# One shared stationary tile for the last 48 columns of gate and up, and a full 128-row last step of down

## The chip, the cores and the metric

The kernel runs on one core of one Trainium2 chip. The metric is the device time of one execution in microseconds (us). Shorter is better. TensorE appears in the profile as PE (matrix products) and PEld (loads of the stationary operand), VectorE as DVE, ScalarE as ACT, GpSimd as POOL, and the queue that issues DMAs as SP.

## What is computed

The kernel holds one layer: a gated delta-rule attention, then a feed-forward part. Input x has 4 sequences of 1024 tokens with 256 values, so 4096 tokens. Cut to the ends and the feed-forward part, the reference is

```python
x = x + _layernorm(attention(_layernorm(x), ...))
x = x + _layernorm(_L0_ffn_ref(_layernorm(x), lut, gate_idx, up_idx, down_idx))

def _L0_ffn_ref(x, lut, gate_idx, up_idx, down_idx):
    gate = x @ lut[gate_idx].T      # 256 -> 688
    up = x @ lut[up_idx].T          # 256 -> 688
    h = silu(gate) * up
    return h @ lut[down_idx].T      # 688 -> 256
```

The layer norm subtracts the mean and divides by the root of the variance plus 1e-5, with no weights. Everything is float32. The 688 columns are five full tiles of 128 and one of 48 (`FT` is 6, `FR` is 48).

## The kernel before

It has two parts with a barrier of all engines between them. The attention runs as a loop of 64 units (16 key heads by 4 sequences), software-pipelined, with each engine's order written out by hand. In its spare places it also turns the 16-entry table and the index arrays into weights: the indices of the three feed-forward weights lie side by side in `widx`, `WCOLS` = 4288 columns on 128 partitions, cut into 16 pieces of `WC` = 268. For each piece DVE makes sixteen products "index equals i, times lut[i]" (`lm`, L896) and POOL adds them up (`la`, L1484); the sum goes to DRAM (`wtd`).

The feed-forward part (from L1620) loads these weights into `ws` with two DMAs and works through 8 blocks of 512 tokens. Four lists of instructions, one for an engine, are tied together by semaphores:

- PE (`ffn_pe`): `gate_up(b, t)` multiplies block b's normalised, transposed tokens (`fxnT`, moving, 512 columns) by tile t of gate (w = 0) and of up (w = 1), each as two products over the two halves of the 256 input values (h). Step i = 6b + t writes gate to one PSUM bank and up to the next: banks strip and emit for even i, ml and mr for odd i. So the last tile, t = 5, is always in ml and mr. `down(b, n)` makes 128 tokens of block b's output, six products of 256 columns summed over the tiles; n = 0, 1 go to bank kv, n = 2, 3 to bank qa. `transposes` makes the next block's `fxnT` through the bank pp.
- ACT (`ffn_act`): `sg` is silu of the gate bank, `xt` copies the transposes, `fo` copies kv or qa to the output tile F.
- DVE (`ffn_dve`): `gate(b, t)` multiplies silu's result by the up bank and writes the tile `hb`. Between these it does the norms: stats and out of the two norms ahead of the products (0 and 1), two blocks early, and of the one behind them (2).
- SP (`ffn_sp`): the loads, and a store of each block once its sum is done.

The order of PE in a block b is gate_up of tiles 0, 1, 2, then down(b-1, 0) and (b-1, 1), gate_up of tiles 3, 4, 5, the transposes of b+1, then down(b-1, 2) and (b-1, 3). A bank is free again when DVE's gate two steps earlier is done:

```python
pe.wait_ge(s["h"], i - 1)
```

DVE does the gate of tile 5 of a block only after the stats of norm 2, which wait for both halves of F of the block before:

```python
dv.wait_ge(s["fo"], 2 * b + 2)
stats(2, b, f.F)
if gates:
    gate(j - 1, 5)
```

So `gate_up(b+1, 1)`, which writes ml and mr again, waits behind that gate, and behind down(b-1, 3), ACT's copy and the stats.

In the build, each product carries the part of the array that it uses as rows by columns. For the 48 columns of the last gate and up tile it is 128 by 64, for the 48-row step of down 64 by 128, and 128 by 128 for every other product of this part. The trace has two PE records for each float32 product: a `down` group of six products is 12 records, two groups are "x24", and one gate or up tile is "x4".

Of the kernel before, what the change touches and what calls it, by code (L numbers as in the profile page):

```python
# [11 lines left out]
ACT = mybir.ActivationFunctionType  # L12
AXIS = mybir.AxisListType

NB, S, HID = 4, 1024, 256
T = NB * S
NT = T // 128
KH, VH, D = 16, 32, 128
# [3 lines left out]
INTER, LUT = 688, 16  # L22
FT = (INTER + 127) // 128
FR = INTER - 128 * (FT - 1)
WCOLS = 4 * INTER + FT * HID
WC = WCOLS // KH
GUK = -(-4 * INTER // WC)
MAGIC = 1597463007.0
EG, NEG, EGLB, EGLS = range(4)
SUB = 62  # L30
# [1596 lines left out]
def ffn_dve(nc, s, g, f, bk):  # L1627
    dv, v = Engine(nc.vector), nc.vector

    def stats(i, j, src):  # L1630
        norm_stats(nc, dv, s, f.st[:, i], f.mv[:, i], f.var[:, i], f.rstd[:, i], f.tn[:, i], src, j,
                   norms_before(i, j))

    def out(i, j, src, fin):
        norm_out(nc, s, f.mv[:, i], f.rstd[:, i], src, fin, j)

    def gate(b, t):
        i = b * FT + t
        rows = 128 if t < FT - 1 else FR
        dv.wait_ge(s["sg"], i + 1)  # L1640
        dv.wait_ge(s["gu"], 2 * i + 2)
        dv.wait_ge(s["dp"], 4 * (b - 1))
        v.tensor_tensor(f.hb[b % 2][0:rows, t, :], bk.all[3 + 2 * (i % 2)][0:rows, :], f.sg[i % 2][0:rows, :],  # L1643
                        ALU.mult).then_inc(s["h"], 1)

    for j in range(10):
        gates = [(j - 1, t) for t in range(FT)] if 1 <= j <= 8 else []
        if gates:
            gate(j - 1, 0)
        if j < 8:  # L1650
            js = slice(4 * j, 4 * j + 4)
            if j < 4:
                dv.wait_ge(s["da%d" % (j // 2)], 16)
            stats(0, j, f.A)
            out(0, j, f.A, f.A)
            if gates:
                gate(j - 1, 1)
            dv.wait_ge(s["xn"], NT + 4 * norms_before(0, j) + 4)
            dv.wait_ge(s[f"x{j // 2}"], 32)
            v.tensor_tensor(f.A[:, js, :], f.A[:, js, :], f.xs[:, js, :], ALU.add).then_inc(s["x1f"], 1)  # L1660
            if gates:
                gate(j - 1, 2)
            dv.wait_ge(s["x1f"], j + 1)
            stats(1, j, f.A)
            out(1, j, f.A, f.xs)
        elif gates:
            gate(j - 1, 1)
            gate(j - 1, 2)
        if gates:
            gate(j - 1, 3)  # L1670
            gate(j - 1, 4)
        if j >= 2:
            b = j - 2
            js = slice(4 * b, 4 * b + 4)
# [4 lines that stand above are left out]
            out(2, b, f.F, f.F)  # L1679
            dv.wait_ge(s["xn"], NT + 4 * norms_before(2, b) + 4)  # L1680
            v.tensor_tensor(f.F[:, js, :], f.F[:, js, :], f.A[:, js, :], ALU.add).then_inc(s["o"], 1)
        elif gates:
            gate(j - 1, 5)


def ffn_pe(nc, s, g, f, bk):
    pe = Engine(nc.tensor)

    def transposes(j):
        for i in (2 * j, 2 * j + 1):  # L1690
            pb = bk.all[i % 2]
            pe.wait_ge(s["xn"], NT + 4 * norms_before(1, j) + 2 * (i % 2) + 2)
            pe.wait_ge(s["xt0"], NT // 2 + i - 1)
            for k in range(2):
                for h in range(2):
                    ins = nc.tensor.transpose(pb[:, (2 * h + k) * 128:(2 * h + k + 1) * 128],  # L1696
                                              f.xs[:, 2 * i + k, h * 128:(h + 1) * 128], g.ident)
            ins.then_inc(s["xtp"], 1)

    def gate_up(b, t):  # L1700
        i = b * FT + t
        rows = 128 if t < FT - 1 else FR
        pe.wait_ge(s["ws"], 16)
        pe.wait_ge(s["xt0"], NT // 2 + 2 * b + 2)
        pe.wait_ge(s["h"], i - 1)
        for w in range(2):
            for h in range(2):
                ins = nc.tensor.matmul(bk.all[2 + 2 * (i % 2) + w][0:rows, :], f.gu[:, w, h, t * 128:t * 128 + rows],  # L1708
                                       f.xnT[:, h, b * 512:(b + 1) * 512], start=h == 0, stop=h == 1)
            ins.then_inc(s["gu"], 1)  # L1710

    def down(b, n):
        pe.wait_ge(s["wsd"], 16)
        pe.wait_ge(s["h"], b * FT + FT)
        pe.wait_ge(s["fo"], 2 * (b - 1) + n // 2 + 1)
        for t in range(FT):
            rows = 128 if t < FT - 1 else FR
            ins = nc.tensor.matmul(bk.all[6 + n // 2][:, (n % 2) * 256:(n % 2) * 256 + 256],  # L1718
                                   f.hb[b % 2][0:rows, t, n * 128:(n + 1) * 128], f.dn[0:rows, t, :],
                                   start=t == 0, stop=t == FT - 1)  # L1720
        ins.then_inc(s["dp"], 1)

    transposes(0)
    for b in range(8):
        for t in range(3):
            gate_up(b, t)
        for n in range(2 if b else 0):
            down(b - 1, n)
        for t in range(3, FT):
            gate_up(b, t)  # L1730
        if b < 7:
            transposes(b + 1)
        for n in range(2, 4 if b else 0):
            down(b - 1, n)
    for n in range(4):
        down(7, n)


def ffn_act(nc, s, g, f, bk):
    ac, a = Engine(nc.scalar), nc.scalar  # L1740

    def xt(j):
        for i in (2 * j, 2 * j + 1):
            ac.wait_ge(s["xtp"], NT // 2 + i + 1)
            a.activation(f.xnT[:, :, i * 256:(i + 1) * 256], bk.all[i % 2][:].rearrange("p (h t) -> p h t", h=2),
                         ACT.Copy).then_inc(s["xt0"], 1)

    def sg(b, t):
        i = b * FT + t
        rows = 128 if t < FT - 1 else FR  # L1750
        ac.wait_ge(s["gu"], 2 * i + 1)
        ac.wait_ge(s["h"], i - 1)
        a.activation(f.sg[i % 2][0:rows, :], bk.all[2 + 2 * (i % 2)][0:rows, :], ACT.Silu).then_inc(s["sg"], 1)

    def fo(b, k):
        ac.wait_ge(s["dp"], 4 * b + 2 * k + 2)
        a.activation(f.F[:, 4 * b + 2 * k:4 * b + 2 * k + 2, :], bk.all[6 + k][:].rearrange("p (c n) -> p c n", c=2),  # L1757
                     ACT.Copy).then_inc(s["fo"], 1)

    xt(0)  # L1760
    for b in range(8):
        for t in range(3):
            sg(b, t)
        if b:
            fo(b - 1, 0)
        for t in range(3, FT):
            sg(b, t)
        if b < 7:
            xt(b + 1)
        if b:  # L1770
            fo(b - 1, 1)
    fo(7, 0)
    fo(7, 1)


def ffn_sp(nc, s, f, dr):
# [9 lines left out]
    xs(0)  # L1786
    ws("ws", 0, GUK)
    nc.sync.dma_start(f.A[:, CH:2 * CH, :], dr.accd[1]).then_inc(s["da1"], 16)
    xs(1)
    ws("wsd", GUK, KH)  # L1790
    xs(2)
    xs(3)
    for b in range(8):
# [15 lines left out]


def program(nc, x, wqkv, wz, wo, convw, wba, dtb, alog, normw, lut, widx,
            c_f32, c_mask, c_gr, c_reset, c_u0, out):
    with ExitStack() as ctx:
        s = {k: ctx.enter_context(nc.semaphore("s_" + k)) for k in SEMS}
# [16 lines left out]
        bk = Bag()  # L1831
# [13 lines left out]
        with ExitStack() as lp:  # L1845
# [47 lines left out]
            p = Bag()  # L1893
# [13 lines left out]
            w = m.NTr[:].rearrange("p u d -> p (u d)")  # L1907
# [12 lines left out]
        with ExitStack() as tmp:  # L1920
            f = Bag()
            f.A = g.A
            f.xnT = alloc(tmp, "fxnT", [128, 2, T])
            f.xs = alloc(tmp, "xs", [128, NT, HID])
            f.F = alloc(tmp, "F", [128, NT, HID])
            f.st = alloc(tmp, "st2", [128, 3, NT, 6])
            f.mv = alloc(tmp, "mv2", [128, 3, NT, 2])
            f.var = alloc(tmp, "var2", [128, 3, NT])
            f.rstd = alloc(tmp, "rstd2", [128, 3, NT])
            f.tn = alloc(tmp, "tn2", [128, 3, NT])  # L1930
            f.ws = alloc(tmp, "ws", [128, WCOLS])
            f.hb = [alloc(tmp, f"hb{i}", [128, FT, 512]) for i in range(2)]
            f.sg = [alloc(tmp, f"sg{i}", [128, 512]) for i in range(2)]
            f.gu = f.ws[:, 0:4 * INTER].rearrange("p (w h n) -> p w h n", w=2, h=2)
            f.dn = f.ws[:, 4 * INTER:].rearrange("p (t n) -> p t n", t=FT)
            ffn_sp(nc, s, f, dr)
            ffn_dve(nc, s, g, f, bk)
            ffn_pe(nc, s, g, f, bk)
            ffn_act(nc, s, g, f, bk)
            nc.all_engine_barrier()  # L1940
# [66 lines left out]
```

## Time and profile before

| | us |
|---|---|
| median of 3 runs | 4693.45 (4693.4 to 4694.74) |
| the profiled execution, its own time | 4695.35 |
| its span, first to last instruction | 4693.2 |
| PE busy in the span | 4520.2 (96%) |
| DVE, ACT, POOL busy | 3785.7, 2890.7, 2698.7 |
| the feed-forward products, first to last | 4378.3 to 4682.2 |

The span is what the profile's rows add up to; the profiled execution's own time is 2.15 us more. Busy shares are averages over the whole span, of which the attention takes more than nine tenths. The feed-forward part is the last 330 us. What bounds it is read from the chain of work that ended last and from the waits in that stretch.

### The profile page before, as it was taken

What the parts mean: (1) busy time and instruction counts of PE and PEld (TensorE: products, weight loads), DVE (VectorE), ACT (ScalarE), POOL (GpSimd) and SP (SyncE); (2) the same over time, 40 slices, a digit from 0 to 9 for tenths busy, and PEclk for the clock granted to TensorE, in tenths of its full rate; (3) what the DMA queues carried; (4) which work ended last, traced back from release to release, by engine and by line L of the source; (5) the groups of instructions that cost most, each with busy time, mean ns of one, the idle gap of its engine ahead of it and who ended that gap; (6) DMA issues with size and microseconds to landing.
All of it is one profiled execution on the core that took longest, in us unless ns stands there. A gap on an engine that the chain in (4) does not pass through costs nothing. (4 is left out here: it accounts for less than half of the span.)

```text
span 4693.2 us, 98481 instructions
## 1 busy us (share of the span) xinstructions
PE 4520.2 (96%) x33236; PEld 3328.1 (71%) x33236; DVE 3785.7 (81%) x8453; ACT 2890.7 (62%) x5548; POOL 2698.7 (58%) x8592
## 2 busy tenths in 40 slices
PE   4899999999999999999999999999999999998798
PEld 2577777777777777777777777777777777776444
DVE  6688888888888888888888888888888888885554
ACT  3466666666666666666666666666666666664111
POOL 1566666666666666666666666666666666664000
PEclk7899999999999999999999999999999999999899
DMA  3212212122121221212222122121221112110200
GB/s 104 43 38 47 49 37 46 38 47 49 37 57 36 49 47 37 48 45 49 47 48 45 39 47 49 37 52 42 47 57 38 43 41 50 43 38 22 69 14 18
DMA packets 575856, 210.05 MB, mean 45 GB/s; under 512 B 455181, under 2 KB 539661, under 8 KB 574329
## 3 DMA queue, kind: packets, MB, share of 16 engines
q1 hardware_dynamic: 574392, 200.48, 18.6%
q8 instruction: 265, 4.34, 0.4%
q0 software_dynamic: 960, 3.28, 0.3%
q14 instruction: 239, 1.95, 0.1%
HBM read 155.84 MB, written 47.81 MB: 43 GB/s over the span
## 5 line engine op out<-in xcount | busy, mean ns | idle before, releaser
L711 DVE SCALAR_TENSOR_TENSOR CV<-pp,CW,CV 128x1023 f32<-128x1023 f32 (+2 forms) x768 | 979.8, 1276 | 33.0 <-ACT CV L1114 22.8
L332 PE MATMUL pp<-A,W 128*128 128x512 f32 x2048 | 962.7, 598 | 9.3 <-DVE CV L711 8.6
L1423 POOL TENSOR_TENSOR TM<-UL,XL 128x126 f32<-128x126 f32 (+22 forms) x1984 | 700.9, 353 | 252.3 <-DMA UL<-c_u 121.7
L1426 POOL TENSOR_TENSOR UL<-UL,TM 128x126 f32<-128x126 f32 (+22 forms) x1984 | 734.2, 370 | 155.4
L332 PEld LDWEIGHTS pp<-A,W 128*128 128x128 f32 x2048 | 373.9, 193 | 305.7 <-issue 294.6
L1202 ACT ACTIVATE QE<-qa,TAB 128x128 f32<-128x128 f32 x1024 | 319.1, 363 | 415.2 <-PE qa L455 413.7
L871 DVE SCALAR_TENSOR_TENSOR CO<-CO,ty,SZ 128x128 f32<-128x128 f32 x1024 | 341.5, 395 | 223.6 <-ACT SZ L1231 216.5
L497 PE MATMUL emit<-Wz,A 128*128 128x256 f32 x2048 | 497.3, 386 | 1.0 <-DVE A L885 1.0
L518 PE MATMUL emit<-Wo,NTr 128*128 128x256 f32 x2048 | 494.2, 384 | 0.8 <-ACT NTr L1247 0.8
L1213 ACT ACTIVATE VS<-qa,EB 128x128 f32<-128x128 f32 x1024 | 319.8, 365 | 224.1 <-PE qa L465 221.8
L834 DVE SCALAR_TENSOR_TENSOR St<-St,TAB,kv 128x128 f32<-128x128 f32 x1024 | 309.9, 344 | 162.0 <-PE kv L474 156.2
L1114 ACT ACTIVATE CV<-pp,CW 128x1024 f32<-128x1024 f32 x256 | 285.3, 1115 | 221.8 <-PE pp L332 220.3
L518 PEld LDWEIGHTS emit<-Wo,NTr 128*128 128x128 f32 x2048 | 376.6, 191 | 58.5 <-issue 13.1
L497 PEld LDWEIGHTS emit<-Wz,A 128*128 128x128 f32 x2048 | 373.6, 190 | 52.5 <-DVE A L885 1.6
L820 DVE SCALAR_TENSOR_TENSOR R<-kv,TAB,V 128x128 f32<-128x128 f32 x1024 | 309.1, 343 | 92.4 <-PE kv L445 90.1
L465 PEld LDWEIGHTS qa<-R,N 128*128 128x128 f32 x2048 | 293.4, 191 | 117.9 <-issue 93.4
L1460 POOL TENSOR_TENSOR tv<-SC,EQ 128x4 f32<-128x4 f32 x256 | 51.2, 200 | 528.6 <-DVE SC L853 528.5
L445 PE MATMUL kv<-St,QK 128*128 128x256 f32 x1024 | 341.1, 415 | 11.7 <-DVE St L834 7.3
L484 PEld LDWEIGHTS qa<-VN,AT 128*128 128x128 f32 x2048 | 303.6, 191 | 65.3 <-ACT VN L1223 24.7
L465 PE MATMUL qa<-R,N 128*128 128x128 f32 x2048 | 329.9, 284 | 4.3 <-ACT QE L1202 4.2
L1239 ACT ACTIVATE JS<-CO 128x512 f32<-128x512 f32 x256 | 160.8, 628 | 274.6 <-DVE CO L845 274.6
L1404 POOL TENSOR_TENSOR tt<-ty 128x4 f32<-128x4 f32 x768 | 159.7, 208 | 292.3 <-DVE ty L861 252.1
(227 smaller groups left out, 9925.6 us busy)
## 6 DMA issues: line engine op xcount, KB each, us to landing
W<-wqkv SPq DMA_DIRECT2D x256, 128.0 KB, 2.6
XL<-xb SPq DMA_DIRECT2D x128, 256.0 KB, 4.0
xb<-X SPq DMA_DIRECT2D x512, 32.0 KB, 1.6
UL<-c_u SPq DMA_DIRECT2D x64, 256.0 KB, 4.2
ub<-UL SPq DMA_DIRECT2D x128, 128.0 KB, 3.1
Wo<-wo SPq DMA_DIRECT2D x64, 256.0 KB, 3.2
N<-ub SPq DMA_DIRECT2D x256, 64.0 KB, 2.2
Wz<-wz SPq DMA_DIRECT2D x64, 256.0 KB, 4.3
```

What stands on the lines that cost most here:

```text
L332: ins = t.matmul(bk.pp[:, 512 * h:512 * h + 512], m.W[:, c, k, :], m.xnT[:, w // KH % 2, c, 512 * h:512 * h + 512], start=c == 0, stop=c == 1)
L445: t.matmul(bk.kv[:, 0:256], m.QK[:, 3 + w % 3, c * 128:(c + 1) * 128], sf, start=True, stop=True).then_inc(s["ks"], 1)
L465: ins = t.matmul(bk.qa[:, 256 + 128 * r:384 + 128 * r], m.N1[w % 2][:, 2 * c + r, :], m.R[k % 2][:, r, :], start=True, stop=True)
L497: ins = t.matmul(bk.out[:, c * 256:(c + 1) * 256], m.xnT[:, w // KH % 2, h, t0:t0 + 128], m.Wz[:, w % 2, h, :], start=h == 0, stop=h == 1)
L518: ins = t.matmul(bk.out[:, c * 256:(c + 1) * 256], m.NTr[:, 2 * c + r, :], m.Wo[:, w % 2, r, :], start=r == 0, stop=r == 1)
L711: v.scalar_tensor_tensor(m.CV[:, t, d:S], bk.pp[:, 0:S - d], m.CW[:, w % KH, t, 3 - d:4 - d], m.CV[:, t, d:S], ALU.mult, ALU.add).then_inc ...
L834: ins = v.scalar_tensor_tensor(m.St[:, r, :], m.St[:, r, :], m.TAB[w % 2][:, EGLS, c, r:r + 1], bk.kv[:, r * 128:(r + 1) * 128], ALU.mult, ...
L871: ins = v.scalar_tensor_tensor(co[:, u, :], co[:, u, :], m.ty[:, u:u + 1], m.SZ[:, u, :], ALU.mult, ALU.mult)
L1202: ins = a.activation(m.QE[:, r, :], bk.qa[:, r * 128:(r + 1) * 128], ACT.Copy, scale=m.TAB[w % 2][:, EG, c, r:r + 1])
L1213: ins = a.activation(m.VS[:, r, :], bk.qa[:, 256 + r * 128:384 + r * 128], ACT.Copy, scale=m.EB[w % 2][:, c, r:r + 1])
L1423: gp.tensor_tensor(m.TM[:, 0:a, 0:b], m.UL[:, 0:a, k:k + 1].to_broadcast([128, a, b]), m.XL[:, k, k + 1:32].unsqueeze(1).to_broadcast([128 ...
L1426: gp.tensor_tensor(m.UL[:, 0:a, k + 1:32], m.UL[:, 0:a, k + 1:32], m.TM[:, 0:a, 0:b], ALU.subtract).then_inc(s["sub"], 1)
```

## The change

The last tile of gate and up becomes one stationary tile of 112 columns: gate's 48 in columns 0 to 47, 16 columns that nothing reads, up's 48 in columns 64 to 111. One pair of products (h = 0, 1) writes both into bank ml, on partitions 0 to 47 and 64 to 111. It counts up the semaphore `gu` by 2 at its end. ACT's silu reads partitions 0 to 47 and writes 64 to 111 of `sg`; DVE's gate multiplies there and writes partitions 64 to 111 of `hb`. Both `hb` tiles get zeros in tile 5 once, by two memsets of DVE in j = 0, ahead of the first gate, and the first gate of tile 5 waits for them (`hz`). down's last step runs over all 128 rows: the weights of its rows 64 to 111 are the real ones, the others are copies of real weights, multiplied by zeros. `WCOLS` goes from 4288 to 4320 and `WC` from 268 to 270.

```diff
--- before.py
+++ after.py
@@ -22,9 +22,12 @@
 INTER, LUT = 688, 16
 FT = (INTER + 127) // 128
 FR = INTER - 128 * (FT - 1)
-WCOLS = 4 * INTER + FT * HID
+GT = 128 * (FT - 1)
+GL = 64
+GC = 2 * GT + GL + FR
+WCOLS = 2 * GC + FT * HID
 WC = WCOLS // KH
-GUK = -(-4 * INTER // WC)
+GUK = -(-2 * GC // WC)
 MAGIC = 1597463007.0
 EG, NEG, EGLB, EGLS = range(4)
 SUB = 62
@@ -1636,11 +1639,13 @@
 
     def gate(b, t):
         i = b * FT + t
-        rows = 128 if t < FT - 1 else FR
+        rows, bank = (slice(0, 128), 3) if t < FT - 1 else (slice(GL, GL + FR), 2)
         dv.wait_ge(s["sg"], i + 1)
         dv.wait_ge(s["gu"], 2 * i + 2)
         dv.wait_ge(s["dp"], 4 * (b - 1))
-        v.tensor_tensor(f.hb[b % 2][0:rows, t, :], bk.all[3 + 2 * (i % 2)][0:rows, :], f.sg[i % 2][0:rows, :],
+        if t == FT - 1:
+            dv.wait_ge(s["hz"], 2)
+        v.tensor_tensor(f.hb[b % 2][rows, t, :], bk.all[bank + 2 * (i % 2)][rows, :], f.sg[i % 2][rows, :],
                         ALU.mult).then_inc(s["h"], 1)
 
     for j in range(10):
@@ -1663,6 +1668,9 @@
             dv.wait_ge(s["x1f"], j + 1)
             stats(1, j, f.A)
             out(1, j, f.A, f.xs)
+            if j == 0:
+                for hb in f.hb:
+                    v.memset(hb[:, FT - 1, :], 0.0).then_inc(s["hz"], 1)
         elif gates:
             gate(j - 1, 1)
             gate(j - 1, 2)
@@ -1699,13 +1707,18 @@
 
     def gate_up(b, t):
         i = b * FT + t
-        rows = 128 if t < FT - 1 else FR
         pe.wait_ge(s["ws"], 16)
         pe.wait_ge(s["xt0"], NT // 2 + 2 * b + 2)
         pe.wait_ge(s["h"], i - 1)
+        if t == FT - 1:
+            for h in range(2):
+                ins = nc.tensor.matmul(bk.all[2 + 2 * (i % 2)][0:GL + FR, :], f.gu[:, h, 2 * GT:GC],
+                                       f.xnT[:, h, b * 512:(b + 1) * 512], start=h == 0, stop=h == 1)
+            ins.then_inc(s["gu"], 2)
+            return
         for w in range(2):
             for h in range(2):
-                ins = nc.tensor.matmul(bk.all[2 + 2 * (i % 2) + w][0:rows, :], f.gu[:, w, h, t * 128:t * 128 + rows],
+                ins = nc.tensor.matmul(bk.all[2 + 2 * (i % 2) + w][:, :], f.gu[:, h, w * GT + t * 128:w * GT + t * 128 + 128],
                                        f.xnT[:, h, b * 512:(b + 1) * 512], start=h == 0, stop=h == 1)
             ins.then_inc(s["gu"], 1)
 
@@ -1714,9 +1727,8 @@
         pe.wait_ge(s["h"], b * FT + FT)
         pe.wait_ge(s["fo"], 2 * (b - 1) + n // 2 + 1)
         for t in range(FT):
-            rows = 128 if t < FT - 1 else FR
             ins = nc.tensor.matmul(bk.all[6 + n // 2][:, (n % 2) * 256:(n % 2) * 256 + 256],
-                                   f.hb[b % 2][0:rows, t, n * 128:(n + 1) * 128], f.dn[0:rows, t, :],
+                                   f.hb[b % 2][:, t, n * 128:(n + 1) * 128], f.dn[:, t, :],
                                    start=t == 0, stop=t == FT - 1)
         ins.then_inc(s["dp"], 1)
 
@@ -1747,10 +1759,10 @@
 
     def sg(b, t):
         i = b * FT + t
-        rows = 128 if t < FT - 1 else FR
+        dst, src = (slice(0, 128), slice(0, 128)) if t < FT - 1 else (slice(GL, GL + FR), slice(0, FR))
         ac.wait_ge(s["gu"], 2 * i + 1)
         ac.wait_ge(s["h"], i - 1)
-        a.activation(f.sg[i % 2][0:rows, :], bk.all[2 + 2 * (i % 2)][0:rows, :], ACT.Silu).then_inc(s["sg"], 1)
+        a.activation(f.sg[i % 2][dst, :], bk.all[2 + 2 * (i % 2)][src, :], ACT.Silu).then_inc(s["sg"], 1)
 
     def fo(b, k):
         ac.wait_ge(s["dp"], 4 * b + 2 * k + 2)
@@ -1805,7 +1817,7 @@
         "sub", "vt", "m1", "y1l", "y1r", "m2", "u12", "v10", "m3", "y2", "m4", "ulr",
         "S0", "ks", "R", "qs", "QE", "vn", "VN", "VS", "sup", "S", "at", "core",
         "z", "SZ", "sq", "red", "tv", "oy", "on", "nrm", "ctp", "NT", "op", "oacc", "ixf", "lm", "la",
-        "da0", "da1", "da2", "da3", "ws", "wsd", "x1f", "gu", "sg", "h", "dp", "fo", "o", "out")
+        "da0", "da1", "da2", "da3", "ws", "wsd", "x1f", "gu", "sg", "h", "hz", "dp", "fo", "o", "out")
 
 
 def program(nc, x, wqkv, wz, wo, convw, wba, dtb, alog, normw, lut, widx,
@@ -1931,8 +1943,8 @@
             f.ws = alloc(tmp, "ws", [128, WCOLS])
             f.hb = [alloc(tmp, f"hb{i}", [128, FT, 512]) for i in range(2)]
             f.sg = [alloc(tmp, f"sg{i}", [128, 512]) for i in range(2)]
-            f.gu = f.ws[:, 0:4 * INTER].rearrange("p (w h n) -> p w h n", w=2, h=2)
-            f.dn = f.ws[:, 4 * INTER:].rearrange("p (t n) -> p t n", t=FT)
+            f.gu = f.ws[:, 0:2 * GC].rearrange("p (h n) -> p h n", h=2)
+            f.dn = f.ws[:, 2 * GC:].rearrange("p (t n) -> p t n", t=FT)
             ffn_sp(nc, s, f, dr)
             ffn_dve(nc, s, g, f, bk)
             ffn_pe(nc, s, g, f, bk)
@@ -1974,11 +1986,12 @@
     z = a["L0_attn_W_z"].reshape(KH, 2 * D, 2, 128).transpose(0, 3, 2, 1)
     o = a["L0_attn_W_out"].reshape(HID, KH, 2, D).transpose(1, 3, 2, 0)
     ba = np.stack([a["L0_attn_W_b"], a["L0_attn_W_a"]]).reshape(2, 32, 2, 128).transpose(3, 2, 0, 1)
-    gu = [a[n].reshape(INTER, 2, 128).transpose(2, 1, 0).reshape(128, 2 * INTER)
-          for n in ("L0_ffn_gate_idx", "L0_ffn_up_idx")]
+    ga, up = (a[n].reshape(INTER, 2, 128).transpose(2, 1, 0) for n in ("L0_ffn_gate_idx", "L0_ffn_up_idx"))
+    gu = np.concatenate([ga[:, :, :GT], up[:, :, :GT], ga[:, :, GT:], ga[:, :, :GL - FR], up[:, :, GT:]], 2)
     dt = a["L0_ffn_down_idx"].T
-    dt = np.concatenate([dt, dt[:FT * 128 - INTER]], 0).reshape(FT, 128, HID).transpose(1, 0, 2).reshape(128, FT * HID)
-    wi = np.concatenate(gu + [dt], 1).reshape(128, KH, WC).transpose(1, 0, 2)
+    dt = np.concatenate([dt[:GT], dt[:GL], dt[GT:], dt[:128 - GL - FR]], 0)
+    dt = dt.reshape(FT, 128, HID).transpose(1, 0, 2).reshape(128, FT * HID)
+    wi = np.concatenate([gu.reshape(128, 2 * GC), dt], 1).reshape(128, KH, WC).transpose(1, 0, 2)
     cf, mask, gr, reset, u0 = consts()
     arrays = {
         "x": a["L0_attn_x"].reshape(T, HID),
```

PE's order, in the build before, from down(b-1, 0) to the first product of the next block:

```order
L1718 MATMUL kv<-ws,hb 128x256 x12
L1708 MATMUL ml<-fxnT,ws 128x512 x2
L1708 MATMUL mr<-fxnT,ws 128x512 x2
L1708 MATMUL strip<-fxnT,ws 128x512 x2
L1708 MATMUL emit<-fxnT,ws 128x512 x2
L1708 MATMUL ml<-fxnT,ws 48x512 x2
L1708 MATMUL mr<-fxnT,ws 48x512 x2
L1696 MATMUL pp<-cf,xs 128x128 x8
L1718 MATMUL qa<-ws,hb 128x256 x12
L1708 MATMUL strip<-fxnT,ws 128x512 x2
```

The shape is that of the result, the count that of products. The same place of PE's order in the changed kernel:

```order
L1730 MATMUL kv<-ws,hb 128x256 x12
L1721 MATMUL ml<-fxnT,ws 128x512 x2
L1721 MATMUL mr<-fxnT,ws 128x512 x2
L1721 MATMUL strip<-fxnT,ws 128x512 x2
L1721 MATMUL emit<-fxnT,ws 128x512 x2
L1715 MATMUL ml<-fxnT,ws 112x512 x2
L1704 MATMUL pp<-cf,xs 128x128 x8
L1730 MATMUL qa<-ws,hb 128x256 x12
L1721 MATMUL strip<-fxnT,ws 128x512 x2
```

Two products of each block are gone, those into mr, and nothing else of PE moved. In the build of the changed kernel every product of this part uses the array as 128 by 128.

DVE's order in the changed kernel, at the end of j = 0:

```order
L107 TENSOR_TENSOR rstd<-rstd,tn 128x4 [waits s_rsq]
L1619 TENSOR_SCALAR xs<-A,mv,rstd 128x256 [waits s_rsq]
L1619 TENSOR_SCALAR xs<-A,mv,rstd 128x256 x3
L1673 MEMSET hb 128x512 x2
L1648 TENSOR_TENSOR hb<-emit,sg 128x512 [waits s_gu,s_sg]
L1607 BN_STATS st<-A 128x6 x4
```

The two memsets stand between the last operation of norm 1 and the first gate; DVE's order is otherwise that of before.

## Rows read from the trace of the kernel before

**Rows 1.** The page: span, and busy time of each engine over it.
```profile
span 4693.2 us, 98481 instructions
...
PE 4520.2 (96%) x33236; PEld 3328.1 (71%) x33236; DVE 3785.7 (81%) x8453; ACT 2890.7 (62%) x5548; POOL 2698.7 (58%) x8592
```

**Rows 2.** Windows, by stage: us of PE, PEld, DVE, ACT, POOL, then granted clock.
```profile
2000.00:3000.00 1000.00, 997.69 (x7754) 752.97 (x7754) 851.49 (x1829) 676.11 (x1301) 643.41 (x2051) 1.00 0.20 46
...
4378.30:4682.20 303.90, 282.11 (x824) 144.82 (x824) 158.37 (x608) 45.17 (x78) 0.00 (x0) 0.96 0.06 21
```

**Rows 3.** The chain that ended last, one block: start us, us, what.
```profile
4495.34 1.91 PE ml L1708 x4
...
4500.69 1.72 PE emit L1708 x4
4502.41 1.85 PE ml L1708 x4
...
4505.97 1.03 PE pp L1696 x8
4507.00 5.78 PE qa L1718 x24
...
4517.94 0.69 DVE hb L1643
```

**Rows 4.** The same chain, other places of the feed-forward part.
```profile
4375.56 1.98 PE pp L1696 x8
...
4399.44 1.92 PE ml L1708 x4
...
4415.41 5.77 PE kv L1718 x24
...
4444.51 1.98 PE ml L1708 x4
...
4480.75 3.09 PE ml L1708 x4
4483.83 2.31 PE mr L1708 x4
...
4655.97 5.98 PE qa L1718 x24
...
4667.84 8.34 PE kv L1718 x24
4676.18 5.98 PE qa L1718 x24
```

**Rows 5.** Timeline of PE from 4489.4: start us, us, instruction, count.
```profile
4489.41 2.32 PE L1718 MATMUL kv<-ws,hb 128*128 128x256 f32 x10
```

**Rows 6.** Timeline of PEld, one of down's groups: what it waited for in brackets.
```profile
4492.29 2.02 PEld L1718 LDWEIGHTS kv<-ws,hb 128*128 128x128 f32 x10 [0.33 <-issue]
4494.65 0.29 PEld L1718 LDWEIGHTS kv<-ws,hb 48*128 48x128 f32 x2 [0.33 <-issue]
```

**Rows 7.** Waits from 4340 to 4694: us in total, times, longest.
```profile
PE ml L1708 <- DVE hb L1643: 15.1, 8, 2.3
```

**Rows 8.** Timeline of DVE: two gates of block 4480.
```profile
4499.08 0.69 DVE L1643 TENSOR_TENSOR hb<-mr,sg 128x512 f32<-128x512 f32 x1 [1.30 <-PE mr L1708]
4502.52 0.69 DVE L1643 TENSOR_TENSOR hb<-emit,sg 128x512 f32<-128x512 f32 x1 [2.74 <-PE emit L1708]
```

**Rows 9.** Timeline of DVE, the first gate.
```profile
4384.17 0.69 DVE L1643 TENSOR_TENSOR hb<-emit,sg 128x512 f32<-128x512 f32 x1 [8.02 <-PE emit L1708]
```

**Rows 10.** Windows of PE: length, busy (x), granted clock, DMA share, GB/s.
```profile
4444.50:4448.00 3.50, 3.50 (x8) 1.00 0.02 5
4480.70:4484.20 3.50, 3.45 (x5) 0.61 0.00 1
```

**Rows 11.** L1484: durations min/median/max in ns.
```profile
L1484 POOL TENSOR_TENSOR wd<-wd,wv x240: 747/752/781, 99.8 to 4225.8; 128x268 f32<-128x268 f32 x120
```

**Rows 12.** L916, a memset of DVE: durations min/median/max in ns.
```profile
L916 DVE MEMSET VL<- x1: 912/912/912, 2.1 to 2.1; 128x1024 f32 x1
```

## The prediction

> **What bounds the kernel now.** I read the busy shares of the page first: PE is busy for 4520.2 of 4693.2 us [rows 1]. The change touches only the feed-forward part and, a little, the table lookups of the attention loop, so the next view is the table of windows [rows 2]. In the loop PE is busy for 997.69 of 1000 us, in the feed-forward part for 282.11 of 303.90, and DVE there for only 158.37. So PE sets the pace in this part too, with short waits. The chain of waits shows how a block closes [rows 3]: PE makes gate and up of tiles 3, 4 and 5, the transposes and two groups of down (qa), then ACT and DVE work in a row up to the gate of tile 5 (4517.94), and PE's next product into ml starts right behind it. PE waited for this gate 8 times, 15.1 us in all, 2.3 us at the longest [rows 7]. All that PE does from one of these gates to the end of qa lies on the path; what it does between the end of qa and the wait (tile 0 of the next block) does not.
>
> The part has 8 blocks. Blocks 1 to 7 hold one pair of kv and qa groups each, and the last pair stands alone at the end.
>
> **Step 1, two products fewer in each block.** A gate or up tile is four records. In a plain place it takes 1.72 us, so 0.429 each (emit at 4500.69) [rows 3]. The shared tile takes four records instead of eight: the moving side is 512 columns as before, and the tile of 48 columns takes no less than one of 128 does. So 1.72 us go in each block, all of it on the path: 8 x 1.716 = **13.7 us**. ACT's silu of tile 5 could start after gate's pair and still can, at the same moment, since the only pair now ends there. DVE's gate of tile 5 is late for another reason (the stats behind qa), so its length and the moved partitions cost nothing; if an operation that writes other partitions than it reads took longer, more than 8 us lie between that silu (about 4504.3) and the gate's start at 4517.94.
>
> **Step 2, the 48-row step of down.** Ten products of 128 rows in a row take 2.32 us [rows 5]. The last is 0.38 long (a sole record's length in this trace), so the distance of two starts is (2.32 - 0.38) / 9 = 0.2157 us. At this pace 24 records take 5.18 us. They take 5.77 and 5.78 [rows 3, 4]. PEld shows where the rest is: between its ten loads of 128 rows there is next to no idle time, but ahead of the loads of the 48-row step, and again ahead of the next ones of 128 rows, it is idle for 0.33 us [rows 6]. So a change of the array's shape costs something each way. Two groups hold three changes inside, 0.59 us together, and the fourth falls on the tile behind them: ml takes 1.91 instead of 1.72, so 0.19 (4495.34) [rows 3]. A group pays 0.39 us for its 48-row step. In the changed kernel every product has the same shape, so all of it goes. On the path this is, for each of the blocks 1 to 7, 0.59 + 0.19 for kv and 0.59 for qa, 1.37 us. The 0.19 behind qa falls on tile 0, ahead of the wait, and only makes the wait longer. 7 x 1.37 = 9.6. At the end kv takes 8.34 at half clock for its first half (I take 0.6 off), and qa 5.98, which holds four changes (5.98 - 5.18 = 0.80) [rows 4]. Together **11.0 us**. The added rows cost nothing by the same rows: a step of 128 rows keeps the pace of 0.2157.
>
> The Trainium skill (TensorEngine Tiling, Key Properties) says that changing the tiling mode drains the engine; it gives no price. From its page TensorE: Matmul & The Clock Gate (Single matmul latency, Back-to-back issue gap) I estimate 163 ns for one drain, the difference of (398 + N) / 2.4 and N / 2.4 + 2.5. By that estimate the two changes of a group would cost 0.33 us, and the whole sum would be 25 us. The rows' 0.39 decides.
>
> **Step 3, the 48-column tile of gate and up.** It uses the array as 128 by 64, and the same kind of change shows: ml takes 1.85 where it would take 1.72, so 0.13 (4502.41) [rows 3]. Behind it the transposes take 1.03. Their undisturbed time is not in the trace. Half of their 1.98 at half clock [rows 4] gives a gain of 0.04, and the 0.19 that a change costs elsewhere gives the other end. I take 0.15, nearer to the second since the same change is made. So 0.28 for each of the blocks 1 to 6. Block 0's tile already stands behind a wait (1.92, against 1.98 for a full tile behind a wait [rows 4]), so about 0.1 there. In block 7 qa stands right behind it (5.98 instead of 5.78), so 0.33. Together **2.1 us** (1.4 to 2.4). The new tile has 112 columns and the shape 128 by 128, so I take it that no change is left; if one is, this term is zero.
>
> **Step 4, small things.** The two memsets stand on DVE ahead of its first gate, where it waits 8.02 us for PE [rows 9]. A memset of twice the columns takes 0.912 us [rows 12], so even two of these are hidden. The cover would be gone only if PE's first tile came 6 us earlier. Zeroed rows are not read by anything else. In the loop 240 additions of POOL go from 268 to 270 columns, 752 ns each [rows 11]: 5.6 ns more, 1.3 us in all over 64 units, and less on DVE. POOL is busy for 643 of 1000 us and DVE for 851, PE for 998 [rows 2], so I take nothing, with 2 us as the bound for the case that each one hit the path. The store and load of the weights grow by 0.7%.
>
> **What is late next.** Within a block DVE could now become the late one. With PE faster by 0.78 in kv and its follower, the gate of tile 3, which waited 1.30 us for PE in this block [rows 8], waits less. That block had lost 1.7 us of clock, so in one at full clock this gate is some 0.4 behind PE already. It holds up only the product of tile 5, which comes 3.43 us (two tiles) after tile 3; 0.78 less leaves over 1 us. So nothing appears in DVE's place, and the wait ahead of ml grows from 2.29 (six of the eight of rows 7) to about 2.5.
>
> **Step 5, the clock.** After the wait at 4444.51 the granted clock is 1.00, the full 2.4 GHz. After the one at 4480.75, just as long, it drops to 1.2 GHz for a stretch, 0.61 on average [rows 10], and ml and mr take 3.09 + 2.31 instead of 1.98 + 1.72: 1.70 us lost [rows 4]. Four of the six waits of this kind lose it in the profiled execution. Same length, different outcome: the trace doesn't say which wait gets it. In the changed kernel six somewhat longer waits stand. Bounds are none and all six, -6.8 and +3.4 us against now; I take four again, as the waits hardly change. The wait of 5.9 us ahead of the last kv stays, and its loss with it.
>
> **The sum.** 13.7 + 11.0 + 2.1 = 26.8 us. The profiled execution's span becomes 4693.2 - 26.8 = 4666.4, its time 4668.5. The median of the runs lies 1.9 us under the profiled one (one clock loss has this size), so from 4693.45 I forecast **4666.6 us**. A measurement of this kernel can tell about 0.2%, 9.4 us, from no change.
>
> **The rivals.**
> - *The clock goes another way*, by at least two waits: 4666.6 - 3.4 to - 6.8, about 4661.5, or + 3.4, 4670. For it: the drops hang on something that identical waits don't show, and all blocks get shorter. Chance 0.18.
> - *The 112-column tile still pays a change of shape*, since its loads differ from those of 128: 4666.6 + 2.1 = 4668.7. Against it: the build's shape is 128 by 128. Chance 0.08.
> - *The gaps come from the end of a sum or the semaphore, not from the shape.* Then step 2 and 3 give nothing: 4693.45 - 13.7 = 4679.7. Against it: the tiles of gate and up end sums with semaphores too and follow each other at 1.72. Chance 0.04.
> - *The change is slower*: longer waits and thinner work of PE in this part keep the clock at 1.2 GHz for most of a block. A block has about 30 us of PE work, which at half clock takes 30 us more, so it decides from one block on: one such block gives 4697, two 4727. Against it: the window of the part has a clock of 0.96 [rows 2], and after each loss it came back within 4 us. Chance 0.01.
>
> **The numbers.** The forecast has 0.69. Faster by over 0.2% are the forecast, the clock, the 112-column and the semaphore rival, 0.97 with a little taken off for what I don't see: 0.96; same 0.025; slower 0.015. The range takes in the clock's cases but for the tail, the 2.1 and the 2 us of the lookups: 4661 to 4673.
>
> **What would show it.** In the profile after: no rows into mr of 48 columns; kv and qa x24 at 5.18 (5.2 for the last qa); ml behind kv at 1.72; the 112-column ml at 1.72 and pp at 0.9; waits of about 2.5 us ahead of ml; a block of 32.9 us at full clock instead of 36.2. I am wrong if x24 stays near 5.8, if gaps appear ahead of tile 5 (DVE late), or if the loop's PE idle grows.

## The result, and the profile after

| | before, us | changed, us |
|---|---|---|
| median of the runs | 4693.42 (4692.95 to 4694.74, 4 runs) | 4668.24 (4667.82 to 4668.7, 4 runs) |
| span of the profiled execution | 4693.2 | 4665.7 |
| feed-forward part: first stats of a norm to the end of the span | 330.1 | 304.6 |
| waits ahead of ml that lost clock | 4 of 6 | 5 of 6 |

The ratio is 0.9944, with a 95% interval of 0.9931 to 0.9958 (the two medians alone give 0.9946). The change took 25.2 us off. The forecast was 4666.6, in a range of 4661 to 4673.

First the page of the changed kernel, its top rows (before: [rows 1]):

```profile
span 4665.7 us, 98419 instructions
...
PE 4492.2 (96%) x33204; PEld 3331.9 (71%) x33204; DVE 3787.8 (81%) x8455; ACT 2890.6 (62%) x5548; POOL 2702.3 (58%) x8592
```

PE has 28 us less to do, the span is 27.5 us shorter. 2.0 of the 27.5 lie ahead of the feed-forward part and have nothing to do with the change (see "The two kernels once more"). The part itself is 25.5 us shorter. Then the windows, the feed-forward products alone (columns as in [rows 2]):

```profile
4378.30:4655.50 277.20, 253.26 (x791) 148.74 (x789) 159.82 (x609) 45.74 (x78) 0.00 (x0) 0.95 0.06 20
```

The chain of waits shows one whole block, from one wait of PE for DVE to the next (start us, us, what; before: [rows 3]):

```profile
4575.33 1.98 PE ml L1721 x4
...
4582.47 5.18 PE kv L1730 x24
4587.65 1.72 PE ml L1721 x4
...
4592.80 1.72 PE emit L1721 x4
4594.51 1.72 PE ml L1715 x4
4596.23 0.87 PE pp L1704 x8
4597.10 5.20 PE qa L1730 x24
...
4607.46 0.70 DVE hb L1648
4608.21 3.22 PE ml L1721 x4
4611.43 2.18 PE mr L1721 x4
```

kv and qa take 5.18 and 5.20 where they took 5.77 and 5.78, ml behind kv 1.72 instead of 1.91. The shared tile takes 1.72, and pp behind it 0.87 instead of 1.03. From 4575.33 to 4608.21 are 32.88 us. The block at full clock before ran from 4444.51 to 4480.75 [rows 4], 36.24 us. The last two rows here are a wait that lost the clock: 3.22 + 2.18 instead of 1.98 + 1.72.

The wait itself grew as PE's tile 0 lost its 0.19 (waits, from 4340 on; before: [rows 7]); the seven are six of 2.49 and one of 0.39, and block 0's wait of 1.0 us is now ahead of L1715:

```profile
PE ml L1721 <- DVE hb L1648: 15.3, 7, 2.5
```

DVE's two memsets take 1.02 us and its wait behind them is 6.75 us where it was 8.02 [rows 9] (timeline of DVE):

```profile
4374.21 1.02 DVE L1673 MEMSET hb<- 128x512 f32 x2
4381.98 0.69 DVE L1648 TENSOR_TENSOR hb<-emit,sg 128x512 f32<-128x512 f32 x1 [6.75 <-PE emit L1721]
```

The gate of tile 3, which waited 1.30 us for PE in a block that had lost clock [rows 8], now waits 0.29 in such a block (timeline of DVE):

```profile
4454.88 0.69 DVE L1648 TENSOR_TENSOR hb<-mr,sg 128x512 f32<-128x512 f32 x1 [0.29 <-PE mr L1721]
```

### The profile page after: what moved, and what is told of

It reads as the page before. It is cut to its first block and busy times, and to the rows that moved or that the text cites. A ratio compares the mean times of both kernels' runs of the same rounds, so it can differ in the third digit from the quotient of the medians.

```text
span 4665.7 us, 98419 instructions
## 1 busy us (share of the span) xinstructions
PE 4492.2 (96%) x33204; PEld 3331.9 (71%) x33204; DVE 3787.8 (81%) x8455; ACT 2890.6 (62%) x5548; POOL 2702.3 (58%) x8592
## 5 line engine op out<-in xcount | busy, mean ns | idle before, releaser
L714 DVE SCALAR_TENSOR_TENSOR CV<-pp,CW,CV 128x1023 f32<-128x1023 f32 (+2 forms) x768 | 979.6, 1275 | 31.6 <-ACT CV L1117 21.4
L335 PEld LDWEIGHTS pp<-A,W 128*128 128x128 f32 x2048 | 373.7, 193 | 305.4 <-issue 294.2
```

The source lines that it names most:

```text
L335: ins = t.matmul(bk.pp[:, 512 * h:512 * h + 512], m.W[:, c, k, :], m.xnT[:, w // KH % 2, c, 512 * h:512 * h + 512], start=c == 0, stop=c == 1)
L714: v.scalar_tensor_tensor(m.CV[:, t, d:S], bk.pp[:, 0:S - d], m.CW[:, w % KH, t, 3 - d:4 - d], m.CV[:, t, d:S], ALU.mult, ALU.add).then_inc ...
```

## The experiments

Between these kernels the feed-forward part differs, and in the attention only the width of the table lookups (268 or 270 columns). The attention ends at another moment in each execution: the stats of the first norm begin at 4363.08 and 4361.08 in the two profiles above, and in the profiles of the nine edited kernels below somewhere from 4360.51 to 4363.86. So next to the medians I give the length of the feed-forward part in the profiled execution, from these stats to the end of the span, and how many of its six waits were followed by products at 1.2 GHz.

| kernel | median, us | part, us | losses of 6 |
|---|---|---|---|
| before | 4693.42 | 330.1 | 4 |
| changed | 4668.24 | 304.6 | 5 |
| down alone | 4682.58 | 317.2 | 3 |
| gate and up alone | 4670.80 | 306.6 | 0 |
| changed, pair twice | 4679.13 | 314.2 | 2 |
| changed, 112 rows | 4668.83 | 304.9 | 5 |
| changed, filled block | 4689.60 | 324.8 | 5 |
| changed, half as much filling | 4669.84 | 305.4 | 0 |
| changed, gate 5 first | 4646.46 | 283.8 | 0 |
| changed, new order of DVE | 4635.27 | 270.5 | 0 |
| before, new order of DVE | 4662.89 | 298.4 | 0 |

A loss means that the products behind a wait took up to 1.7 us longer, at the lower clock. In the three kernels at the bottom the six long waits are gone or shorter, as told below. The kernel before was timed again beside each group of edited kernels, with medians from 4693.48 to 4694.52 us; the ratios below are against those.

**The two kernels once more.** No edit; one profile of each.

> The kernel before once more. Theory (the clock loss falls on waits by the moment, not by the wait): of the six waits of 2.29 us ahead of ml between 3 and 6 lose 1.7 us, perhaps others than in the first profile; the span ahead of the feed-forward part differs by up to 2 us from the first profile's. Rival: the same four waits lose it again.

> The changed kernel once more. Theory: between 3 and 6 of the six waits of 2.5 us lose 1.7 us of clock, and all else of the feed-forward part is as in the first profile to 0.1 us. Rival: the same five waits again.

Before took 4695.85, the changed kernel 4670.4. The feed-forward parts came out at 330.1 and 304.7 us, as the first time, and the same four waits and the same five lost the clock. So the rival holds in both: what was unequal between executions is the attention, not this. The chain of before, second profile:

```profile
4445.00 1.98 PE ml L1708 x4
...
4481.24 3.12 PE ml L1708 x4
4484.36 2.27 PE mr L1708 x4
...
4519.16 3.50 PE ml L1708 x4
```

Where the attention differs can be read too. PE's first product of line 393 (396 in the changed kernel), early in the attention, is already 2.25 us later in the first profile of before than in that of the changed kernel (timeline of PE, before and then changed):

```profile
168.78 0.21 PE L393 MATMUL ml<-VL,X 32*32 32x32 f32 x1 [0.91 <-DVE VL L782]
166.53 0.21 PE L396 MATMUL ml<-VL,X 32*32 32x32 f32 x1 [0.91 <-DVE VL L785]
```

From this product to the first stats of the norm all thirteen profiles take 4194.2 to 4195.3 us. Ahead of it, between 40 and 175 us, the granted clock is 0.67 on average in the first profile of before and 0.70 in the first of the changed kernel. Three groups of products into pp there take 6.59, 5.80 and 5.37 us in the one and 5.76, 5.37 and 5.19 in the other, 1.4 of the 2.25 us. So the executions part ways in their first 170 us, for the most part by PE's clock. The timed runs agree, though for them only a mean clock is known: of the 40 of the kernel before beside the experiments, the 16 with a mean granted clock of 0.981 took 4694.49 to 4696.14 us, the 20 with 0.983 took 4692.7 to 4694.4, and the four with 0.982 lie from 4692.63 to 4694.45.

**Down alone.** The kernel before with down's last step over 128 rows:

```diff
-            rows = 128 if t < FT - 1 else FR
             ins = nc.tensor.matmul(bk.all[6 + n // 2][:, (n % 2) * 256:(n % 2) * 256 + 256],
-                                   f.hb[b % 2][0:rows, t, n * 128:(n + 1) * 128], f.dn[0:rows, t, :],
+                                   f.hb[b % 2][:, t, n * 128:(n + 1) * 128], f.dn[:, t, :],
```

with the two memsets and their wait of the change.

> The kernel before with one part of the change: down's last step runs over 128 rows (zeros in rows 48 to 127 of hb); gate and up of tile 5 stay two pairs of 48 columns. Theory (a change of the array's shape costs 0.1 us each way): the 24-record groups go from 5.78 to 5.2 us, the ml tile behind kv from 1.91 to 1.72, ml of tile 5 stays at 1.85 and pp at 1.03; 11.0 us less, 4682.4, within 3.4 for the clock. Rival (the gaps come from the end of a sum or its semaphore): 24 records stay at 5.78, 4693.4.

It took 4682.58 us, ratio 0.9974 (0.9964 to 0.9985). One block of its chain:

```profile
4523.58 5.18 PE kv L1722 x24
4528.76 1.72 PE ml L1713 x4
...
4533.91 1.72 PE emit L1713 x4
4535.63 1.85 PE ml L1713 x4
4537.47 1.72 PE mr L1713 x4
4539.19 1.02 PE pp L1701 x8
4540.21 5.20 PE qa L1722 x24
```

kv is at 5.18 and its follower at 1.72, while tile 5 still shows 1.85 and pp 1.02. The second tile of 48 columns (mr) follows a product of its own shape and takes 1.72, no more than a full one: it is the change that costs, not the small product. The part is 12.9 us shorter, of which one clock loss fewer is 1.7, so 11.2 for the shape changes of down against 11.0 in the theory. (0.5 of it lie in block 0 ahead of its tile 5, where down has no part; the last kv gave 0.3 where the theory took 0.6.) The rival is out.

**Gate and up alone.** The changed kernel with the real rows only in down:

```diff
         for t in range(FT):
+            rows = slice(0, 128) if t < FT - 1 else slice(GL, GL + FR)
             ins = nc.tensor.matmul(bk.all[6 + n // 2][:, (n % 2) * 256:(n % 2) * 256 + 256],
-                                   f.hb[b % 2][:, t, n * 128:(n + 1) * 128], f.dn[:, t, :],
+                                   f.hb[b % 2][rows, t, n * 128:(n + 1) * 128], f.dn[rows, t, :],
```

> The changed kernel with down's last step over its 48 real rows alone (partitions 64 to 111, array shape 64 by 128 at row 64). Theory: the shape changes are back, 24 records at 5.78 and the ml tile behind kv at 1.91; 11.0 us more than the changed kernel, 4679.2, within 3.4 for the clock; ml of the shared tile stays at 1.72 and pp at 0.87. Rival (only a tile at row 0 pays, or the price was that of loading few rows at partition 0): 4668.

It took 4670.80 us, ratio 0.9949 (0.9935 to 0.9964). That is below the forecast with its 3.4 us for the clock, and near the rival's number. But the rows side with the theory:

```profile
4507.82 1.98 PE ml L1721 x4
...
4514.95 5.77 PE kv L1731 x24
4520.72 1.91 PE ml L1721 x4
...
4527.78 1.72 PE ml L1715 x4
4529.50 0.87 PE pp L1704 x8
4530.37 5.78 PE qa L1731 x24
...
4541.32 0.70 DVE hb L1648
4542.06 1.98 PE ml L1721 x4
```

kv is back at 5.77, its follower at 1.91, and a block takes 34.24 us (4507.82 to 4542.06) instead of 32.88. What was not in my sum is the clock: none of the six waits is followed by half clock here (the ml tiles take 1.98 each time), where the changed kernel lost 8.2 us. 11.0 more for the shape and 8.2 less for the clock make 2.8, and 2.6 were measured. Against before, without clock losses on either side, the part is 330.1 - 6.8 - 306.6 = 16.7 us shorter, where the theory's terms give 13.7 + 2.1 = 15.8. The 0.9 between them is the last kv, which stands behind the wait of 5.9 us: it took 7.51 us here and 8.34 before, with the same shape changes in it.

**The pair twice.** The changed kernel with the shared pair made first into mr, for nobody, and then into ml:

```diff
-            for h in range(2):
-                ins = nc.tensor.matmul(bk.all[2 + 2 * (i % 2)][0:GL + FR, :], f.gu[:, h, 2 * GT:GC],
-                                       f.xnT[:, h, b * 512:(b + 1) * 512], start=h == 0, stop=h == 1)
+            for w in range(2):
+                for h in range(2):
+                    ins = nc.tensor.matmul(bk.all[3 - w + 2 * (i % 2)][0:GL + FR, :], f.gu[:, h, 2 * GT:GC],
+                                           f.xnT[:, h, b * 512:(b + 1) * 512], start=h == 0, stop=h == 1)
```

> The changed kernel with the shared pair made twice, first into mr (which nobody reads then), then into ml: work doubled, shape kept. Theory: 8 x 1.716 = 13.7 us more than the changed kernel, 4681.9, within 3.4 for the clock, with both pairs at 1.72 and no other gap. Rival (part of the pair was hidden behind DVE's gate of tile 3 or another wait): less than 8 us more.

It took 4679.13 us, ratio 0.9967 (0.9954 to 0.9979), 10.9 more than the changed kernel. Each pair takes 1.72 and nothing hides either. The two losses left cost 3.4 us where the changed kernel's five cost 8.2, so 4.8 of clock are to be added to the part's 9.6: 14.4. The last kv has to come off. Its 24 records are the same in both kernels, and so is the wait of 5.92 us ahead of it, but it took 0.64 longer here (chain of waits, pair twice and then changed):

```profile
4652.62 8.27 PE kv L1731 x24
4641.91 7.63 PE kv L1730 x24
```

14.4 - 0.6 = 13.8 us for the doubled pair, for 13.7 in the theory.

**112 rows.** The changed kernel with rows 0 to 111 in down's last step (`rows = 128 if t < FT - 1 else GL + FR`, `[0:rows, ...]`).

> The changed kernel with down's last step over rows 0 to 111: fewer rows than 128, but the array shape stays 128 by 128. Theory (shape is what costs): no change, 4668.2, 24 records at 5.18 to 5.20. Rival (any change of the number of rows costs the gap): 11 us more, 4679, 24 records at 5.78.

4668.83 us, ratio 0.9946 (0.9931 to 0.996), the part at 304.9 and kv at 5.19. Fewer than 128 rows cost nothing as long as the build gives the product the shape 128 by 128. So it is not any number of rows below 128 that costs; the 112 columns of the shared tile show it for columns. No run has between 48 and 112 of either, and none gives a product of 48 rows the full shape. The five losses are not at the same waits as in the changed kernel: here the fourth of the six waits kept the clock, there the fifth, though a block is 32.88 us long in both.

**Gate 5 first.** The wait ahead of ml comes from DVE's order, so this moves it:

```diff
             gate(j - 1, 4)
+            gate(j - 1, 5)
...
             stats(2, b, f.F)
-            if gates:
-                gate(j - 1, 5)
...
-        elif gates:
-            gate(j - 1, 5)
```

> The changed kernel with DVE's gate of tile 5 ahead of the stats of norm 2 instead of behind them. Theory (the waits ahead of ml come from that order, and a clock loss needs such a wait): the six waits of 2.5 us ahead of ml and the 5.9 us ahead of the last kv vanish. PE then waits for gate 0 of the next block, which DVE reaches about 8.5 us after qa, where PE wants it at 6.9: six waits of 1.6. So 6 x 0.9 + 5.9 = 11.3 us less, and 0 to 11 us of clock losses less: 4646 to 4657. Rival (the waits only move to the same length elsewhere): 4662 to 4668.

4646.46 us, ratio 0.99 (0.9885 to 0.9915), 21.8 less than the changed kernel. PE now waits for gate 0 of the next block, ahead of strip, six times 1.73 us where 1.6 were expected (waits, from 4380 on):

```profile
PE strip L1718 <- DVE hb L1648: 10.4, 6, 1.7
```

The clock stayed at full speed through all six blocks. 6 x 0.76 of waits, 5.9 ahead of the last kv and 8.2 of clock at the six waits are 18.7. The last kv, which lost clock in the changed kernel (7.63 us), takes 5.18 here, 2.4 less. Together 21.1, for 20.8 in the part.

**The new order of DVE.** Gate 5 first again, and two more gates moved:

```diff
-        if gates:
-            gate(j - 1, 0)
+        if j == 1:
+            gate(0, 0)
...
             stats(1, j, f.A)
+            if gates:
+                gate(j - 1, 3)
             out(1, j, f.A, f.xs)
...
-        if gates:
             gate(j - 1, 3)
+        if j == 1:
+            gate(0, 4)
+            gate(0, 5)
+            gate(1, 0)
+        elif gates:
             gate(j - 1, 4)
+            gate(j - 1, 5)
...
             stats(2, b, f.F)
-            if gates:
-                gate(j - 1, 5)
+            if j < 8:
+                gate(j, 0)
             out(2, b, f.F, f.F)
...
-        elif gates:
-            gate(j - 1, 5)
```

> As gate 5 first, and also gate 0 of the next block ahead of norm 2's out, and gate 3 ahead of norm 1's out. Theory: PE has no wait over 1 us left in a block, a block takes 30.4 to 31.5 us, and the granted clock stays at full speed through blocks 2 to 7: about 15 + 5.9 us of waits and 8 to 11 us of clock less than the changed kernel, 4636 to 4643. Rival (DVE becomes the bound, with 22 us of work and the waits on PE between): 4648 or more.

4635.27 us, ratio 0.9876 (0.986 to 0.9893): 33.0 less than the changed kernel, just under the forecast 4636 to 4643. A block has no wait left at all and takes 30.12 us, where the forecast was 30.4 to 31.5 (chain of waits):

```profile
4431.92 1.72 PE strip L1726 x4
...
4442.22 5.18 PE kv L1735 x24
4447.40 1.72 PE ml L1726 x4
...
4454.27 1.72 PE ml L1720 x4
4455.98 0.87 PE pp L1709 x8
4456.86 5.18 PE qa L1735 x24
4462.04 1.72 PE strip L1726 x4
```

DVE is not the bound; PE is busy for 241.92 of 244 us (windows, PE first, granted clock third from the end):

```profile
4376.00:4620.00 244.00, 241.92 (x789) 145.05 (x788) 158.99 (x610) 46.37 (x79) 0.00 (x0) 0.99 0.08 26
```

This is the version that beats both. It is the change and DVE's order together, which the next run takes apart.

**Before, in the new order.** The kernel before with the same moves on DVE.

> The kernel before with DVE's new order alone (gate 5 and gate 0 early, gate 3 ahead of norm 1's out), so PE has no waits in a block. Against the same order with the change (4635.3) every gap of the shape counts, the 0.19 ahead of tile 0 too. Theory (the savings are PE time and add up): 13.7 + 2.3 + 7 x 1.57 + 1.4 = 28.4 us more, 4663.7, at an unchanged clock. Rival (much of the change's gain in the first measurement came from the clock or the waits): less than 25 us more.

4662.89 us, ratio 0.9931 (0.9914 to 0.9948). Against the same order with the change that is 27.6 us more (27.9 in the part), for 28.4 in the theory, with no clock loss in the blocks of either. A block takes 33.68 us here (4438.11 to 4471.79 in the chain) and 30.12 there. So with waits and clock taken out of the comparison the change is worth 27.6 us, and the rival is out. The new order is worth 31.6 us to the kernel before (4694.52, timed beside it; 31.7 in the part).

**The filled block.** Why gate and up alone lost no clock was open: the shape changes, or the length of a block. This gives the changed kernel longer blocks at an unchanged shape, in blocks 1 to 7:

```diff
         if t == FT - 1:
+            for h in range(4 if b else 0):
+                nc.tensor.matmul(bk.all[3 + 2 * (i % 2)][0:GL + FR, 0:404], f.gu[:, h % 2, 2 * GT:GC],
+                                 f.xnT[:, h % 2, b * 512:b * 512 + 404], start=h % 2 == 0, stop=h % 2 == 1)
```

> The changed kernel with four unused products of 404 columns into mr ahead of tile 5 in blocks 1 to 7: 1.37 us more PE work in each, 9.6 in all, at the same array shape, so that a block is as long as in the kernel whose down kept its 48 rows (34.25 us), which lost no clock. Theory (which waits lose the clock depends on the length of a block, not on the shape changes): no clock loss at the six waits of 2.5 us, so 9.6 - 8.2 = 1.4 more than the changed kernel, 4669.6. Rival (the shape changes kept the clock up): five losses stay, 4677.8.

4689.6 us, 21.4 more than the changed kernel: both expectations missed, because I had sized the filling at half of what it is. The four products take 2.71 us, not 1.37 (chain of waits):

```profile
4535.60 2.71 PE mr L1715 x8
4538.31 1.72 PE ml L1718 x4
```

7 x 2.71 = 19.0 us of work and five clock losses again, in a block of 35.6 us. On the question it was made for the run says only that longer blocks alone don't keep the clock up. And it gives the size for the next one: a product of 404 columns takes 0.68 us.

**Half as much filling.** `range(2 if b else 0)` in the place of 4.

> As the filled block, with two unused products of 404 columns instead of four: the trace of that run shows 0.68 us for one, so two add 1.36 us in blocks 1 to 7, 9.5 in all, and a block is 34.25 us long, as in the kernel whose down kept its 48 rows. Theory (which waits lose the clock depends on the length of a block): no loss at the six waits, 9.5 - 8.2 = 1.3 more than the changed kernel, 4669.5. Rival (the shape changes kept the clock up): five losses stay, 4677.7.

4669.84 us, ratio 0.9948 (0.9931 to 0.9964), the forecast within 0.4. The waits are as long as in the changed kernel, but ml behind them takes 1.98 or 1.99 each time, and a block lasts 34.24 us:

```profile
4542.75 0.71 DVE hb L1648
4543.50 1.98 PE ml L1724 x4
...
4576.98 0.71 DVE hb L1648
4577.73 1.98 PE ml L1724 x4
```

9.5 us more work cost 1.6 us (0.8 in the part). None of the four timed runs is over 4671.08, so none had the five losses, which would have made it 4677.7. It is not the shape changes that kept the clock up. The clock behind the last kv's wait went its own way: that kv took 7.01 us, against 7.63 in the changed kernel (chain of waits):

```profile
4645.32 7.01 PE kv L1733 x24
```

## Why the prediction was right

- **What bounds the part.** Right: PE's work from one gate of tile 5 to the end of qa, then ACT and DVE. The chain after has the same members in the same order. One reading was loose: of the eight waits in [rows 7] only six are for the gate of tile 5; the other two, 0.39 and 0.99 us, are for earlier gates in block 0. The sum used six.
- **Step 1, 13.7 us.** Right. Doubling the pair gave 13.8 once the clock is set aside, and each pair is 1.72 in the rows.
- **Step 2, 11.0 us.** Right: 11.2 by the run with down alone, and kv, its follower and qa came out at 5.18, 1.72 and 5.20. What the term took for the last kv came out by luck: 0.6 expected, 0.71 measured (8.34 to 7.63), but this kv, with the same 24 records and the same wait, took anything from 7.01 to 8.33 in the kernels whose down has no change of shape. The estimate worked out from the Trainium skill (TensorE: Matmul & The Clock Gate, Single matmul latency and Back-to-back issue gap), 0.33 us for a group, would have made the sum 2 us short; the rows' 0.39 was the better one.
- **Step 3, 2.1 us.** Right. pp behind the shared tile takes 0.87, so its share was 0.16 of a range from 0.04 to 0.19. That a tile of 112 columns pays no change of shape holds.
- **The rest by blocks.** Between the products that open each block the savings are 1.84 us in block 0, 3.35 in block 1, 3.36 in each of blocks 2 to 6 at full clock, 3.39 in block 7 and 1.49 at the end: 26.9 us in all, where the sum had 26.8.
- **Step 4.** The memsets are hidden (6.75 us of wait remain). The additions on POOL went from 752 to 759 ns. The loop's PE stayed at 997.7 of 1000 us, and from line 393 (396) on the attention took 4194.3 and 4194.4 us in the two profiles of before, 4194.5 and 4194.7 in those of the changed kernel.
- **What is late next.** Right: no wait on DVE took over, and the waits ahead of ml are 2.49 where I had about 2.5.
- **Step 5, the clock: the term that was off.** I took four losses again and got five, 8.2 us instead of 6.8. 26.9 - 1.4 = 25.5, which is by how much the part shrank. This is the difference of 1.6 us between forecast and result, within the bounds given. The four timed runs of the changed kernel, of which the profiled one is the first, lie within 0.9 us, less than one loss. The remark that the profiled execution of before was 1.9 us slow, about one clock loss, was right in size, but it doesn't lie at the six waits, where the second profile lost the same four: the executions differ in the first 170 us. That the profiled span came out at 4665.7, only 0.7 from the forecast 4666.4, is luck: 2.0 us less of such a start against 1.4 more at the waits.

The rival of a clock that goes another way, priced for at least two waits, came by one wait only. Those of the 112-column tile and the end of a sum are out by the rows above. The slower one (half clock through whole blocks) never showed: behind the six waits no loss was larger than 1.7 us.

## What to carry to other kernels

Look through the build for products that use another shape of the array than their neighbours. Here a way in and out of another shape cost 0.39 us in down, and padding with zeros up to the same shape was free here. Two narrow products over the same moving data can share one stationary tile. And ask of each wait of PE what order on another engine makes it: moving three gates on DVE gave more (33.0 us on top of the change, 31.6 without it) than the change itself (25.2). Where a kernel waits, compare the length of the part in the profile too, and look behind each wait for the clock: gate and up alone lost 11 us to the changed kernel by its rows, and 2.6 us by its median.

## What the runs showed of the hardware

- A product with 48 rows (shape 64 by 128) or 48 columns (128 by 64) costs time on the way in and on the way out, between products of the full shape: 0.19 us each way for the rows, 0.13 and 0.16 for the columns. One with 112 rows or 112 columns (128 by 128) costs none, and neither does a second product of 48 columns behind the first. The Trainium skill (TensorEngine Tiling, Key Properties) says that a change of the tiling mode drains TensorE. The trace agrees in so far as each change costs a pause, and puts 0.39 us on the two changes of a group.
- Where the 48 rows lie doesn't matter: at partitions 64 to 111 kv took 5.77, as at 0 to 47.
- The loss of clock behind a wait of PE is not drawn anew each time. The two profiles of before lost it at the same waits, and so did the two of the changed kernel. With waits of 2.3 to 2.5 us, kernels whose block at full clock is 34.2 us long lost it 0 times of 6, in both cases; at 32.9 us 5 times (two kernels), at 34.6 twice, at 34.9 three times, at 35.6 five times, at 36.2 four times. The length of a block is not all: the two kernels at 32.9 us lost it at different waits. So an edit of a few tenths of a microsecond in a block can come with 1.7 us more or less for each block, and its effect on the clock can be larger than its own. With waits of 1.73 us (gate 5 first, blocks of 32.1 us) there was no loss in six; whether that is the shorter wait or the length no run separates. Why a length is a good or a bad one no run here settles.
- Behind a wait of 5.9 us the same 24 records took from 7.01 to 8.33 us, against 5.18 at full clock.
- Two executions of the changed kernel differ by 2.6 us, and in their profiles PE is 2.4 us apart already at 170 us, with a mean granted clock of 0.70 and 0.67 up to there.
- A float32 product shows as two records. At the full 2.4 GHz these come 0.34 us apart for 404 columns and 0.429 for 512, which is two cycles for each column.
- Zeros in the operands changed nothing in the pace: kv's records with zero rows keep the 0.216 us of the others.
